# Graph attention on one core: adjacency bytes turned by DMA transposes, first tile projected in two parts, first row spread by repeated columns

## What is computed

```python
seq = (x @ W_seq).reshape(N, H, DH)          # N 2048, H 16, DH 32
score1 = jnp.einsum('nhd,d->hn', seq, a1)
score2 = jnp.einsum('nhd,d->hn', seq, a2)
scores = score1[:, :, None] + score2[:, None, :]
scores = jax.nn.leaky_relu(scores, negative_slope=ALPHA)
scores = scores + (1.0 - adj)[None, :, :] * MASK_VAL
attn = jax.nn.softmax(scores, axis=-1)
hidden = jnp.einsum('hij,jhd->ihd', attn, seq).reshape(N, D_IN)
hidden = hidden @ W_out + b_out
out = layernorm(x + jax.nn.elu(hidden))
```

## Time and profile before

| | us |
|---|---|
| median of 3 runs | 549.42 |
| lowest and highest run | 545.85, 550.5 |
| the profiled execution | 546.6 |
| its span, first to last instruction | 544.7 |
| PE busy in the span | 511.0 (94%) |
| DVE busy | 492.1 (90%) |
| ACT busy | 446.8 (82%) |

### The profile page before, as it was taken

One profiled execution on the slowest core, in us unless ns is written; L12 is line 12 of the kernel. 1 busy time (PEld: TensorE's weight loads), 2 busy tenths in 40 slices (PEclk: granted clock), 3 DMA queues, 4 the chain that ended last, 5 costly groups with the idle time before them and its releaser, 6 DMA issues.

```text
span 544.7 us, 15410 instructions
## 1 busy us (share of the span) xinstructions
PE 511.0 (94%) x6813; PEld 459.1 (84%) x6813; DVE 492.1 (90%) x762; ACT 446.8 (82%) x454; POOL 33.7 (6%) x64
## 2 busy tenths in 40 slices
PE   4999997679999999999999999999999999989993
PEld 3788884679999999999999999999999999734441
DVE  6688787998999989999999999999999879989886
ACT  1868686989998989999999999999997868146663
POOL 5000000000000000000000000000000000024542
PEclk9999999589999999999999999999999999999998
DMA  7998601002202011010220102202012040014443
GB/s 256 421 401 296 248 2 64 22 2 78 79 2 79 20 63 78 2 79 2 79 80 1 80 2 79 78 3 80 2 79 79 1 137 4 2 53 136 140 135 116
DMA packets 13334, 48.56 MB, mean 89 GB/s; under 512 B 1428, under 2 KB 2452, under 8 KB 9300
## 3 DMA queue, kind: packets, MB, share of 16 engines
q1 hardware_dynamic: 13268, 47.59, 24.1%
HBM read 43.25 MB, written 4.33 MB: 87 GB/s over the span
## 4 chain that ended last, share of the span: by engine, by line
PE 70%; ACT 14%; DVE 11%; issue 2%; DMA 1%; SPq 1%; POOLq 0%; POOL 0%; DVEq 0%; ACTq 0%
PE sums L358 31%; PE bank L370 17%; ACT tring L515 9%; PE sums L291 9%; PE sums L420 8%; DVE tring L732 3%; DVE tring L718 2%; DMA Vp<-in_adj_dram 1%; PE bank L301 1%; ACT low L504 1%; PE sums L279 1%; DVE Vp L679 1%; PE bank L410 1%; DVE xp L673 1%; PE sums L334 1%
## 5 line engine op out<-in xcount | busy, mean ns | idle before, releaser
L515 ACT ACTIVATE tring<-abc,ab 128x2048 int8<-128x2048 f32 x157 | 305.5, 2023 | 0.0
L358 PE MATMUL sums<-Vp,tring 128*128 128x132 f16 x4096 | 246.2, 223 | 13.1 <-DVE Vp L679 5.5
L358 PEld LDWEIGHTS sums<-Vp,tring 128*128 128x128 fp8e4 x4096 | 241.4, 99 | 15.9 <-issue 10.2
L732 DVE TENSOR_TENSOR tring<-adj,tring 128x512 uint32<-128x512 uint32 x256 | 166.3, 682 | 9.2 <-ACT tring L515 9.1
L370 PE MATMUL bank<-Vp,adj 128*128 128x132 f16 x2048 | 126.1, 221 | 0.7 <-DVE Vp L679 0.7
L718 DVE TENSOR_SCALAR tring<-abc,ab 128x2048 int8<-128x2048 f32 x99 | 126.5, 1277 | 0.0
L370 PEld LDWEIGHTS bank<-Vp,adj 128*128 128x128 fp8e4 x2048 | 122.1, 96 | 1.3 <-DVE Vp L679 1.1
L291 PE MATMUL sums<-Vp,abc 128*128 128x272 f32 x256 | 63.5, 402 | 0.0
L420 PE MATMUL sums<-abc,Vp 128*128 128x512 f32 x128 | 57.7, 595 | 1.3 <-ACT Vp L546 1.3
L291 PEld LDWEIGHTS sums<-Vp,abc 128*128 128x128 f32 x256 | 48.9, 196 | 9.6
L420 PEld LDWEIGHTS sums<-abc,Vp 128*128 128x128 f32 x128 | 23.1, 190 | 25.4 <-issue 23.6
(11 more groups left out here) (77 smaller groups left out, 314.7 us busy)
## 6 DMA issues: line engine op xcount, KB each, us to landing
Vp<-in_adj_dram SPq DMA_DIRECT2D x16, 1024.0 KB, 8.2
abc<-a_rows SPq DMA_DIRECT2D x15, 1024.0 KB, 4.6
abc<-in_x_dram SPq DMA_DIRECT2D x16, 256.0 KB, 5.9
Vp<-in_x_dram SPq DMA_DIRECT2D x16, 256.0 KB, 2.9
out_dram<-Vp SPq DMA_DIRECT2D x16, 256.0 KB, 2.1
Vp<-in_L_gnn_W_seq_dram SPq DMA_DIRECT2D x4, 256.0 KB, 3.7
abc<-in_L_gnn_W_out_dram SPq DMA_DIRECT2D x1, 1024.0 KB, 5.4
Vp<-in_L_gnn_b_out_dram SPq DMA_DIRECT2D x1, 256.0 KB, 5.8
```

The lines of the kernel that those rows point to most:

```text
L358: mm = pe.matmul(bank[b][:, c * 2 * VW:(c + 1) * 2 * VW], slot(jt)[:, it * P:(it + 1) * P].bitcast(F8), Vp[:, h, jt, :, :], start=(jt == 0 ...
L515: act.activation(slot(jt), row(h), ACT.Sign, bias=ab[:, jt, H + h:H + h + 1], scale=-1.0).then_inc(u_ready, 1)
L732: dve.tensor_tensor(words, adj8[:, jt, :].bitcast(U32), words, ALU.bitwise_and).then_inc(t_ready, 1)
```

## The change

- The adjacency bytes are turned by a DMA with transpose, from `tring` to a new ring of four buffers `pairs` in SBUF, issued on SP behind load_adj(t + 3). PE has no turn_adj any more. DVE and ACT copy the turned bytes from SBUF. No bias is added or subtracted.
- The first tile is projected in two parts: 256 columns of each half at once, the 16 score columns of each half behind the second tile's projection. Two of the four loads of W_seq are issued by ACT. The score vectors are negated where they are copied, so both blocks of scores are taken out by one copy, as are the maxima and the projection.
- The first head's row comes from PE transposes of one score column repeated 128 times. All scores are turned in four transposes later, in the first head, and stored in another layout of a_rows.
- The maximum over 15 tiles is taken ahead of the last tile. The spread product reads the maxima repeated instead of a diagonal. The exponentials of heads 1 to 15 move into the first head. The reciprocal of a power of two is made by flipping its exponent bits.
- Three quarters of the first mask of ACT and of DVE are made ahead. The first head's values come in 4 and 12 tiles instead of 8 and 8, and those of heads 1 to 3 at other places.

The diff, cut:

```diff
+PARTS = (slice(0, 4), slice(4, NT))
+SOON = 3 * N // 4
...
-VALUES_AT = ((0, 5, 10),) + ((1,),) * (H - 1)
-HIGH_AT = ((3, 8, 13),) + ((6,),) * (H - 1)
-LOW_AT = ((5, 10, 14),) + ((9,),) * (H - 1)
+VALUES_AT = ((3, 7, 11),) + ((1,),) * (H - 1)
+HIGH_AT = ((5, 9, 13),) + ((6,),) * (H - 1)
+LOW_AT = ((6, 10, 14),) + ((9,),) * (H - 1)
...
+        def wait_turned(eng, it):
+
+            eng.wait_ge(adj_turned[it % TURNED], 16 * (it // TURNED + 1))
...
+            def turn_adj(it):
+
+                sp.wait_ge(adj_fixed, it + 1)
+                if it >= TURNED:
+                    sp.wait_ge(adj_ready[it % 2], (it - TURNED) // 2 + 1)
+                sp.dma_start(pairs[:, it % TURNED], tring[:, it, :].bitcast(F16), transpose=True).then_inc(adj_turned[it % TURNED], 16)
+
             for t in range(NT):
                 load_adj(t)
+                if t >= STAGE - 1:
+                    turn_adj(t - STAGE + 1)
                 if t + XS - 2 < NT:
...
+            for t in range(NT - STAGE + 1, NT):
+                turn_adj(t)
+
+            sp.wait_ge(a_copied, 1)
+            sp.dma_start(scratch.rearrange("(g p) n -> p g n", p=P), aT.rearrange("p (g n) -> p g n", n=P)).then_inc(a_stored, 16)
+            sp.wait_ge(a_stored, 16)
...
-                    if t == 0:
+                    if t == 0 and columns.start == 0:
+                        pe.wait_ge(w_loaded[k], 16)
+                    if t == 1:
                         pe.wait_ge(wa_ready, 2 * k + 2)
...
-            def turn_adj(it):
-                r = it % 2
-                pe.wait_ge(adj_fixed, it + 1)
-                if it >= 2:
-                    pe.wait_ge(adj_ready[r], it // 2)
-                for q in range(NT // 2):
-                    mm = pe.transpose(bank[6 + r].bitcast(F16)[:, q * P:(q + 1) * P],
-                                      tring[:, it, 2 * q * P:2 * (q + 1) * P].bitcast(F16), idh)
-                mm.then_inc(adj_turned, 1)
...
+            def spread_row0(c, tiles):
+
                 for t in tiles:
-                    mm = pe.transpose(turned_a[t // 4][0:H, t % 4 * P:(t % 4 + 1) * P], ab[:, t, 0:H], idf)
+                    mm = pe.transpose(row0_bank[c][:, t % 4 * P:(t % 4 + 1) * P], ab[:, t, 0:1].to_broadcast([P, P]), idf)
                     if t % 4 == 3:
-                        mm.then_inc(a_turned, 1)
+                        mm.then_inc(row0_spread, 1)
 
...
             turn_x(0)
-            for t in range(NT - 2):
+            project(0, slice(0, half))
+            turn_x(1)
+            turn_x(2)
+            project(1)
+            project(0, slice(half, WC)).then_inc(seq_made, 2)
+            turn_x(3)
+            project(2).then_inc(seq_made, 1)
+            for t in range(3, NT - 2):
                 turn_x(t + 1)
-                project(t)
-                turn_adj(t)
+                project(t).then_inc(seq_made, 1)
             turn_x(NT - 1)
             pe.wait_ge(x_copied, NT - 1)
-            turn_a(range(0, 4))
-            project(NT - 2)
-            turn_adj(NT - 2)
-            turn_adj(NT - 1)
-            pe.wait_ge(a_copied, 1)
-            turn_a(range(4, 8))
+            pe.wait_ge(ab_copied, 12)
+            spread_row0(0, range(0, 4))
+            project(NT - 2).then_inc(seq_made, 1)
+            pe.wait_ge(row0_copied, 1)
+            spread_row0(1, range(4, 8))
             pe.wait_ge(x_copied, NT)
-            turn_a(range(8, 12))
-            project(NT - 1)
-
-            def spread_row0(c):
-
-                pe.wait_ge(a_copied, c + 1)
-                pe.matmul(spread_a[c], ones[0:1, :], aT[0:1, c * 512:(c + 1) * 512], start=True, stop=True).then_inc(row0_spread, 1)
-
-            pe.wait_ge(seq_copied, NT - 1)
-            spread_row0(0)
-            turn_a(range(12, 15))
+            spread_row0(2, range(8, 12))
+            project(NT - 1).then_inc(seq_made, 1)
+            pe.wait_ge(row0_copied, 2)
+            pe.wait_ge(ab_copied, NT - 1)
+            spread_row0(3, range(12, 15))
             pe.wait_ge(ab_copied, NT)
-            turn_a(range(15, NT))
-            spread_row0(1)
+            spread_row0(3, range(15, NT))
+
             pe.wait_ge(mx_ready, 1)
-            pe.wait_ge(adj_ready[0], NT // 2)
             pe.transpose(bank[6][0:2 * H, 0:P], mx, idf).then_inc(mx_turned, 1)
-            spread_row0(2)
-            pe.wait_ge(diag_ready, 1)
-            pe.matmul(bank[6][:, 0:2 * H], ones[0:2 * H, :], diag[0:2 * H, :], start=True, stop=True).then_inc(mx_spread, 1)
-            spread_row0(3)
+            pe.wait_ge(mcol_ready, 1)
+            pe.matmul(Mps, mcol[0:2 * H, :].to_broadcast([2 * H, P]), idf[0:2 * H, 0:2 * H], start=True, stop=True).then_inc(mx_spread, 1)
+            for g in range(4):
+                mm = pe.transpose(bank[7][:, g * P:(g + 1) * P], ab[:, 4 * g:4 * (g + 1), :].rearrange("p t c -> p (t c)"), idf)
...
+                wait_turned(act, it)
+                act.copy(adj8[:].rearrange("p (q s) n -> p q s n", s=2)[:, :, :, it * P:(it + 1) * P], turned_pairs(it)).then_inc(adj_ready[1], 1)
...
             copy_row0(2)
+            copy_adj(NT - 1)
+
+            def sign(h, jt, columns=slice(0, N)):
+                return act.activation(slot(jt)[:, columns], row(h)[:, columns], ACT.Sign, bias=ab[:, jt, H + h:H + h + 1], scale=-1.0)
+
+
+            act.wait_ge(row0_copied, 3)
+            act.wait_ge(ab_copied, 1)
+            slot_free(act, 0, 0)
+            sign(0, 0, slice(0, SOON))
             copy_row0(3)
 
...
+                        sign(h, jt, slice(SOON, N) if h == 0 and jt == 0 else slice(0, N)).then_inc(u_ready, 1)
                     if h == 0 and jt == 0:
-                        split_high(0, slice(0, NT // 2))
-                        split_high(0, slice(NT // 2, NT))
-                    if h == 0 and jt == 3:
+                        split_high(0, PARTS[0])
+                    if h == 0 and jt == 2:
+                        split_high(0, PARTS[1])
+                        factors(1, slice(1, H))
+                        act.wait_ge(a_turned, 1)
+                        act.copy(aT, bank[7]).then_inc(a_copied, 1)
+                    if h == 0 and jt == 5:
                         act.wait_ge(r_in, 1)
...
+                dve.tensor_reduce(nbs[:, t, :].rearrange("p (s h) -> p s h", s=2),
+                                  projected(t, slice(0, half)).rearrange("p s (h d) -> p s h d", d=DH), AX.X, ALU.max,
+                                  apply_absolute_value=True).then_inc(mx_part, 1)
...
+                wait_turned(dve, it)
+                dve.tensor_copy(adj8[:].rearrange("p (q s) n -> p q s n", s=2)[:, :, :, it * P:(it + 1) * P], turned_pairs(it)).then_inc(adj_ready[0], 1)
...
+                if t == NT - 1:
+
+                    dve.wait_ge(row0_copied, 3)
+                    slot_free(dve, 0, 1)
+                    above_row(0, 1, slice(0, SOON))
                 copy_ab(t)
...
-            dve.tensor_reduce(mx, mxc.rearrange("p c k -> p k c"), AX.X, ALU.max).then_inc(mx_ready, 1)
+                if t % 4 == 3 and t < NT - 1:
+                    largest(t // 4, slice(t - 3, t + 1))
+                if t == NT - 2:
+                    largest(3, slice(t - 2, t + 1))
+                    dve.wait_ge(mx_part, NT - 1 + 8)
+                    dve.tensor_reduce(most, mxc.rearrange("p c k -> p k c"), AX.X, ALU.max).then_inc(most_ready, 1)
...
+            dve.wait_ge(most_ready, 1)
+            dve.wait_ge(ab_copied, NT)
+            dve.scalar_tensor_tensor(out=mx[:, 0:H], in0=ab[:, NT - 1, H:2 * H], scalar=-1.0, in1=most[:, 0:H],
...
+            dve.tensor_tensor(mx[:, H:2 * H], nbs[:, NT - 1, :], most[:, H:2 * H], ALU.max).then_inc(mx_ready, 1)
             copy_seq(NT - 1)
             dve.wait_ge(mx_turned, 1)
             dve.tensor_reduce(mcol[0:2 * H, :], bank[6][0:2 * H, 0:P], AX.X, ALU.max).then_inc(mcol_ready, 1)
-            dve.wait_ge(mcol_ready, 1)
-            dve.tensor_scalar(diag[0:2 * H, :], idf[0:2 * H, 0:2 * H], mcol[0:2 * H, :], None, ALU.mult).then_inc(diag_ready, 1)
             dve.wait_ge(mx_spread, 1)
-            dve.tensor_copy(Mb, bank[6][:, 0:2 * H]).then_inc(Mb_ready, 1)
-            dve.wait_ge(Mb_ready, 1)
...
+            wait_turned(dve, NT - 1)
+            dve.tensor_tensor(E[:, :, 0, 0:1], ab[:, :, H:H + 1], Mps[:, 0:1].unsqueeze(1).to_broadcast([P, NT, 1]), ALU.add).then_inc(e_in, 1)
...
+            dve.tensor_scalar(vinv.bitcast(U32), vsc[:].bitcast(U32), EXPONENT, EXPONENT, ALU.bitwise_and, ALU.bitwise_xor).then_inc(vsc_step, 1)
+            dve.tensor_scalar(vsc[:].bitcast(U32), vsc[:].bitcast(U32), EXPONENT, None, ALU.bitwise_and).then_inc(vsc_step, 1)
+            dve.tensor_copy(Mb, Mps[:, 0:H]).then_inc(Mb_ready, 1)
+            Mrow = Mb.unsqueeze(1).to_broadcast([P, NT, H])
...
+                        split_low(0, PARTS[0])
+                    if h == 0 and jt == 1:
+                        values(0, PARTS[1])
```

(7 more changed lines are left out.)

172 lines of the change are left out of this document (70 added, 102 removed).

## The result

| | before | after |
|---|---|---|
| median, us | 548.57 (4 runs) | 675.71 (4 runs) |
| lowest and highest run | 545.85, 550.5 | 673.72, 680.43 |
| span of the profiled execution | 544.7 | 671.5 |
| ratio, with its 95% interval | | 1.234 (1.229 to 1.239) |

The changed kernel is 127 us slower. The forecast was 540, its range 535 to 557, and not one of the rivals was it. Some executions of a kernel run slow as a whole (one of the kernel before, at 669.79 us, and one of e9, at 571.95, whose profile is of that one), and medians, ranges and ratios here are of the others. In the kernel after, mask_products is line 376, adj_products 392, project 322, the AND of DVE 765, and the Sign of ACT 488.

What follows compares the result with a forecast made beforehand. PE bounds the projection loop and DVE paces the first head; gains of 5.7 (loop), 2.1 (to scaling) and 0.2 (first head) sum to 8.0 us: 538.6, or 541.4 on the runs' median; forecast 540, range 535 to 557.

Steps and rivals of the forecast that it cites:

- the sentence on the rows: Row loads for later heads: 512-byte pieces cost nothing, having some 22 us; even 15 us would hide.
- The first head's end: Last AND of the first head on DVE: 8.0 us earlier, near 114, 0.2 us of it from the head itself.
- The tail: From the last projection's end to DVE's scaling: 4.0 us instead of 6.1, a gain of 2.1 us.
- The pitch of the loop: Projection loop on PE: 4.12 us a tile without byte turning, before 4.56; loop ends at 81.6 against 87.3.
- rival 1: Projection loop: transposes land late, ACT and DVE stall, five stalls of about 0.9 us; about 545; chance 0.21.
- a share below 0.9 after 45 us: Sign of being right: DMA engines' share in the projection loop below 0.9 after 45 us.
- T: Time one 256 KB DMA transpose keeps the 16 engines: taken at 0.8 us, free to 1.0, whole gain lost at 1.75.
- ACT's and DVE's copies: Copies of turned bytes in the loop: taken as equal from on-chip memory or PSUM, ACT 1.87 us, DVE 2.28.
- Rival 2: Projection loop: transposes fill the DMA engines, T over 1.75; 552 upwards, most around 562; chance 0.22.
- Rival 3: First head does not take the front's gain, ACT coming last; 543; counted within the forecast's 0.57.

Runs made afterwards that it cites:

- e9: The kernel before, with only its row store and row loads cut in 1 KB pieces (1024 a load): 563.19 us, ratio 1.029.
- e1: The changed kernel with the old a_rows layout again (16 whole rows, loaded in 8 KB pieces), the rest of the change kept: 541.2 us, ratio 0.989.
- e6: e1 with eight buffers for turned bytes, DVE copying tiles 0 to 14 one tile later and ACT tile 15 alone: 541.65 us, ratio 0.988.
- e5: e1 with the adjacency bytes turned on PE again, with the bias of 64 and the copies from PSUM: 544.72 us, ratio 0.994.
- e12: e6 with tile 13's turned bytes also copied by ACT instead of DVE: 538.37 us, ratio 0.983.

## Why the prediction was wrong

**The step that failed** is the sentence on the rows: "The rows for later heads now travel in 512-byte pieces instead of 8 KB ones, but have a head's time (some 22 us) against 4.6 us before; I cost it at nothing, and even 15 us would hide." It asked one question, whether the row is there when its head wants it. By that question it was nearly right: the load took 19.1 us where 15 were allowed, and ACT waited 0.5 us for rows in the whole run. It didn't ask who else needs the DMA engines meanwhile. I had named the cover for the row's own consumer and none for PE's instruction queue, which stands in the third part of the page of the kernel before:

```profile
q8 instruction: 53, 0.87, 0.6%
```

The cost was 104 us of stops and 28 us of lower clock.

The 15 us had no row behind it either. The nearest one in my own list, a store of 32 KB in pieces, 1.6 us, would have given some 50 us for 1 MB in proportion. I used that row as the upper bound for the transpose, and not for the load that really was cut in small pieces.

**The rest of the change** can be read apart from this. Lines of the kernel after that answer to the earlier trace rows:

```profile
84.65 0.19 DVE L626 COPY ab<-sums 128x32 f32<-128x32 f32 x1 [0.45 <-PE sums L322]
...
87.75 0.49 DVE L697 SCALAR_TENSOR_TENSOR Es<-tring,Vp 128x16 f32<-128x16 f32 x2 [0.19 <-ACT tring L501]
...
115.66 0.68 DVE L765 TENSOR_TENSOR tring<-adj,tring 128x512 uint32<-128x512 uint32 x1
```

- *The first head's end.* Forecast 8.0 us earlier, at about 114. The last AND of the first head begins at 115.66, 5.75 us before the 121.41 of the earlier trace rows. e1 then measured 541.2; the forecast was 540. That they lie so near is in part luck: the sum was some 2.3 us too hopeful here, and 1.4 us had been put on top of its 538.6 for another reason, the spread of the runs.
- *The tail* was forecast at 4.0 us from the last projection (6.1 before). It ends at 84.6, scaling begins at 87.75: 3.1 us. Right in kind, 0.9 us too careful.
- *The pitch of the loop* was forecast at 4.12 us. project(3) begins at 26.74, so the start did not lose the 0.7 us that I had (27.5); project(14) begins at 76.24. Less the 0.5 us of the first row that is (76.24 - 26.74 - 0.5) / 11 = 4.45, and the last projection ends 3.0 us later than forecast. Most projections stand 4.1 to 4.3 us apart, and three gaps are 5.35, 4.94 and 5.35. This is rival 1, which I had as five stalls and 545 as a whole: transposes that land late. The groups by line of 20 to 80 us, and the windows of the loop and of its end:

```profile
L468 ACT COPY adj<-Vp 128x2048 int8<-128x2048 int8 x7 | 13.3, 1898 | 12.1 <-DMA Vp<-tring 12.1
...
L646 DVE COPY adj<-Vp 128x2048 int8<-128x2048 int8 x7 | 8.5, 1219 | 0.0
```

```profile
20.00:76.00 56.00, 52.10 (x252) 42.53 (x252) 35.16 (x77) 42.46 (x45) 0.00 (x0) 1.00 1.08 341
76.00:80.00 4.00, 4.00 (x21) 3.32 (x20) 3.57 (x7) 4.00 (x5) 0.00 (x0) 1.00 0.35 70
```

ACT stood 12.1 us at the turned bytes, in order before its x copy, and PE was busy 52.1 of 56 us. A transpose landed in 7.3 us (median of all 16), and its issue held SP for 2.9 us (median), which I had at nothing. The engines' share was 1.08 over the loop, against 0.75 in the earlier trace rows. I had named a share below 0.9 after 45 us as a sign of being right; it was 1.10 over 45 to 67 and 0.99 over 67 to 76.
- *The DMA transpose's price* T, taken at 0.8. In a stretch at the loop's end, 76 to 80 us, almost nothing moves but one transpose; DMA queues and issues of it (packets, MB, share):

```profile
q1 hardware_dynamic: 1056, 0.26, 34.0%
...
Vp<-tring SPq DMA_TRANSPOSE x2, 3.0
```

0.26 MB moved in 1056 packets of some 250 bytes, at a share of 0.35 of 4 us: T is about 1.4, an estimate, above the 1.0 that I called free and below the break-even of 1.75. A tile would then keep the engines for 3.1 + 1.4 = 4.5 us, which is the pitch measured. But e6 had its projections 4.11 us apart with the same 16 transposes and a share of 1.10, so what set the pitch was the copies' wait; whether their engine, their later place or the eight buffers did it was not tried apart. e5 agrees in sign: turning by DMA gains some 3 us, not the whole 0.45 us a tile (7.2).
- *ACT's and DVE's copies* I took as equal whether from PSUM or SBUF. ACT's is (1.90 for 1.87), DVE's took 1.22 for 2.28. e6 and e12 rest on that.
- *Rival 2*: its sign came, engines full through the loop, and its price of 562 did not. *Rival 3* did not occur: the scaling came 5.6 us earlier and the last AND of the first head 5.75, so the head took what the front gained.

What stays open: q8's packets show that the fetch comes only at the end of a row load, with the engines shown busy 0.3 meanwhile, but not what holds it back inside them. Nor was it tried how short a load in 1 KB or 512 B pieces has to be for PE not to stop.

## What to carry to other kernels

Ask of every transfer not only whether its own consumer can wait, but what else needs the DMA engines while it runs; a program long enough to be fetched in blocks is one of these. Keep a broadcast from DRAM in few large pieces (here 2 KB or more), or shorter than the time in which PE works through a block. When PE idles for "issue", count its matmuls from stop to stop, and lay the landings of the DMAs and the packets of the instruction queue beside them. Stops of one length at one place of each head are another thing: look there for a semaphore wait that the profile did not name.
